# A two-direction state-space scan with MLP and attention: one four-column sum moved from VectorE to GpSimd, and the scan's last sums reordered on TensorE

## The reference

```
h = (x - mean) * rsqrt(var + 1e-5) * (1 + scale) + shift        # per token, modulated by the condition
for direction in (forward, backward in time):
    xs, z = split(h @ in_w); xs = silu(xs)
    proj = xs @ xproj_w;  dt = softplus(proj[:512] + bias);  B, C = proj[512:576], proj[576:640]
    for each time step:  state = state * exp(dt * A) + dt * xs * B        # 512 channels x 64 states
                         y = sum over the 64 states of state * C
    y = (y + xs * D) * silu(z) @ out_w
x = x + gate * (y_forward + y_backward)
x = x + gate * mlp(norm(x))                                     # then an attention layer with its own MLP
```

## Time and profile before

| what | value |
|---|---|
| median of 3 runs | 3260.04 us (3252.33 to 3261.91) |
| the profiled execution's own time | 3261.6 us |
| its span, first to last instruction | 3258.6 us |
| TensorE matmul busy | 3193.8 us (98%) |
| VectorE busy | 2771.5 us (85%) |
| ScalarE busy | 2679.6 us (82%) |
| GpSimd busy | 2448.3 us (75%) |
| mean granted TensorE clock | 0.994 |

### The profile page before, as it was taken

The page is one execution under the profiler, slowest core; times in us unless marked ns, Lnnn a source line. Parts: engine busy times, 40 slices in busy tenths (PEclk is TensorE's granted clock), DMA queues, the critical chain, the costliest instruction groups (busy, mean ns, idle before and its releaser), DMA issues. The chain is left out here.

```text
span 3258.6 us, 60423 instructions
## 1 busy us (share of the span) xinstructions
PE 3193.8 (98%) x23784; PEld 2687.1 (82%) x23784; DVE 2771.5 (85%) x3073; ACT 2679.6 (82%) x4456; POOL 2448.3 (75%) x617
## 2 busy tenths in 40 slices
PE   8999999999999999999999999999999999999999
PEld 6999899984699989997479999999648999888844
DVE  3999999966399999996659999999656999999861
ACT  4999999955699999994569999999357999999744
POOL 3999999950299999994039999999305999999800
PEclk9999999999999999999999999999999999999999
DMA  5222222210222222220022322222002222222100
GB/s 191 73 81 73 83 73 80 79 46 1 73 72 87 78 84 74 76 85 30 14 81 65 88 79 77 82 73 79 21 14 85 85 76 84 68 74 74 48 14 7
DMA packets 194235, 222.08 MB, mean 68 GB/s; under 512 B 77336, under 2 KB 149016, under 8 KB 193056
## 3 DMA queue, kind: packets, MB, share of 16 engines
q1 hardware_dynamic: 193952, 218.22, 22.1%
HBM read 213.70 MB, written 4.48 MB: 67 GB/s over the span
## 5 line engine op out<-in xcount | busy, mean ns | idle before, releaser
L621 POOL TENSOR_TENSOR states<-states,c_rows 128x2048 f32<-128x2048 f32 x336 | 1533.5, 4583 | 421.1 <-DVE states L1504 417.9
L1504 DVE TENSOR_TENSOR_SCAN states<-decay,bank 128x512 f32<-128x512 f32 x1376 | 1580.8, 1203 | 124.9 <-PE bank L1025 105.9
L771 ACT ACTIVATE decay<-dt,a_log 128x512 f32<-128x512 f32 x2048 | 1308.5, 712 | 0.0
L765 ACT ACTIVATE inflow_tok<-dtx_tok,b_tok 128x512 f32<-128x512 f32 x1536 | 999.2, 715 | 127.5 <-PE bank L1025 121.9
L1024 PE MATMUL bank<-ident,inflow_tok 128*128 128x128 f32 x6144 | 1046.4, 279 | 33.4 <-DVE states L1504 19.2
L1024 PEld LDWEIGHTS bank<-ident,inflow_tok 128*128 128x128 f32 x6144 | 706.5, 141 | 206.1 <-issue 72.1
L1044 PE MATMUL bank<-ident,states 128*128 128x128 f32 x5504 | 825.5, 273 | 4.1 <-DVE y_gated L1510 3.0
L1025 PE MATMUL bank<-b_diag,dtx_tok 128*128 128x128 f32 x4096 | 794.0, 276 | 0.0
L1504 DVE TENSOR_TENSOR_SCAN y_gated<-decay,bank 128x512 f32<-128x512 f32 x672 | 778.2, 1203 | 17.4 <-ACT decay L771 5.0
L621 POOL TENSOR_TENSOR y_gated<-y_gated,c_rows 128x2048 f32<-128x2048 f32 x168 | 770.2, 4584 | 27.9 <-DVE y_gated L1504 26.1
L1044 PEld LDWEIGHTS bank<-ident,states 128*128 128x128 f32 x5504 | 646.3, 142 | 10.5 <-DVE y_gated L1510 5.3
(11 more groups left out here) (161 smaller groups left out, 2238.9 us busy)
## 6 DMA issues: line engine op xcount, KB each, us to landing
c_rows<-c_spill SPq DMA_DIRECT2D x256, 512.0 KB, 3.7
b_diag<-diag_ring SPq DMA_DIRECT2D x256, 128.0 KB, 2.2
xproj_w<-in_xproj_w SPq DMA_DIRECT2D x32, 320.0 KB, 4.1
in_w<-in_in_w SPq DMA_DIRECT2D x16, 512.0 KB, 4.8
in_w<-in_fc_w SPq DMA_DIRECT2D x8, 512.0 KB, 4.4
xproj_w<-in_w SPq DMA_DIRECT2D x8, 512.0 KB, 4.5
xproj_w<-in_fc_w SPq DMA_DIRECT2D x4, 1024.0 KB, 5.3
x_ahead<-in_x SPq DMA_DIRECT2D x4, 512.0 KB, 6.6
```

The costliest lines, as they stand in the source:

```text
L621: pool.tensor_tensor(state_row, state_row, c_row.to_broadcast([P, KI, L]), ALU.mult).then_inc(weighed, PAIRS)
L765: last_tok = act.activation(inflow_tok[:, r % SLOTS, t, :], dtx_tok[:, d, t, :], ACT.Copy, scale=b_tok[:, d, t, s:s + 1])
L771: act.activation(decay[:, r % SLOTS * KI + k, :], dt[:, d, k, :], ACT.Exp, scale=a_neg[:, d, k, s:s + 1]).then_inc(decay_ready, 1)
L1504: dve.tensor_tensor_scan(state_slots[r % STATES][:, k, time], decay[:, slot, time], banks[k % INFLOW_BANKS][:, time], 0.0, ALU.mult, ALU.a ...
```

## The change

It has two parts. The look-ahead's sum of variance and epsilon leaves VectorE's `look_ahead` and is issued by GpSimd's `look_ahead` at the same step number, 16, with the wait for the four aggregates before it. And at the scan's end TensorE's order becomes: two of the four products of `project(0, 0)`, the last step's four `sum_up`, the other two products of `project(0, 0)`, then for each t `turn_high(t)` followed by one product of `project(0, 1)`, then `project(1, t)` as before. The first piece of the diff is in GpSimd's block, the next two in TensorE's, the last in VectorE's.

```
             def look_ahead(b, s):
 
+                if s == AHEAD_VAR_AT:
+                    pool.wait_ge(ahead_aggr, (b + 1) * TT)
+                    pool.tensor_scalar(var_eps[:], mean_var[:, :, 1], EPS_MAMBA, None, ALU.add).then_inc(ahead_var, 1)
                 if s == AHEAD_POWER_AT:
...
-            def project(d, t):
-                for k in range(KI):
+            def project(d, t, tiles=range(KI)):
+                for k in tiles:
                     last = pe.matmul(banks[t][:, 0:D], y_chan[d][:, k, t * P:(t + 1) * P], out_w[:, d, k, :],
...
-                project(0, 0)
-                sum_up(b, r, 0)
-                sum_up(b, r, 1)
-                sum_up(b, r, 2)
-                sum_up(b, r, 3)
-                project(0, 1)
+                project(0, 0, range(0, PAIR))
+                for k in range(KI):
+                    sum_up(b, r, k)
+                project(0, 0, range(PAIR, KI))
                 for t in range(TT):
                     turn_high(b, t)
+                    project(0, 1, (t,))
                 for t in range(TT):
                     pe.wait_ge(y_high_ready, b * TT + t + 1)
                     project(1, t)
...
-                if s == AHEAD_VAR_AT:
-                    dve.wait_ge(ahead_aggr, (b + 1) * TT)
-                    dve.tensor_scalar(var_eps[:], mean_var[:, :, 1], EPS_MAMBA, None, ALU.add).then_inc(ahead_var, 1)
```

## The result

| | before | after |
|---|---|---|
| median of the runs, us | 3260.34 (20 runs, 3252.33 to 3267.41) | 3249.85 (20 runs, 3244.45 to 3255.50) |
| the profiled execution, us | 3261.6 | 3253.48 |
| its span, us | 3258.6 | 3251.7 |
| ratio after / before | | 0.9967, 95% interval 0.9960 to 0.9973 |

The changed kernel is 10.5 us faster by the medians, and 8.8 to 13.0 us by the interval (3260.34 times 0.0027 and 0.0040). The interval lies on both sides of the border of 0.3% that the prediction drew (a ratio of 0.9970): that the kernel is faster is clear, that it is so by more than 0.3% is not.

A forecast was written before the change was run, and what follows sets the result against it. TensorE, busy 98% of the span, was taken to bound the kernel, with VectorE and GpSimd nearly as full. Terms -11.3 + 0 + 1.1 = -10.2 us, from the median 3260.04, gave 3249.8 us, range 3245 to 3256.

The forecast's parts named there:

- the border of 0.3%: Line between faster and the same: a measurement can tell about 0.3%, 9.8 us, from no change; it lies at 3250.3 us.
- Term 1, the gap: Steps 16 to 22, forward: taking the sum off VectorE saves 3.75 us in each of three samples, 11.3 us.
- Term 2, the sum on GpSimd: Step 16, between two GpSimd products: the sum takes 0.2 us, covered by idle time, so 0 us.
- The idle time of 0.33: GpSimd's idle time in us per step before its products, said to cover the sum's 0.2 us.
- the upper end of 1.04: Longest duration in us allowed for the sum on GpSimd, from the four-column power; said to stay covered.
- GpSimd then has no idle time for many steps: Behind step 16, if the sum takes its upper end: GpSimd's backlog is 0.7 us, with step 24 the tightest row.
- The rival in which GpSimd becomes the bound: Sum held on GpSimd for 2.25 us, TensorE waits about 1 us in each of three samples: 3252.8 us; chance 0.06.
- Term 3, the scan's end: TensorE's new order at four scan ends gains nothing and makes the first turn wait: 1.1 us lost, ends 0 and 2.0.
- The rival in which the end pays 0.86 each: Each of four scan ends gives back 0.86 us and no wait arises: 3245.3 us; chance 0.10.
- a wait that costs the clock: At each of four scan ends the wait drops TensorE to half clock, costing 3.75 us: 3263.7 us; chance 0.04.
- Only VectorE's own time returns: In the scan, only 2.25 us a sample comes back, 6.8 us in all: 3254.3 us; chance 0.12.
- The split between faster and the same: Outcome chances around 3250.3 us: faster 0.50, same 0.46; the forecast's 0.68 was divided into 0.40 and 0.28.

The follow-up runs named there:

- e3: Kernel before, with the sum still on VectorE but placed behind the scan of tile 3 of step 16: 3250.84 us, ratio 0.9968.
- e4: Kernel before, with the sum still on VectorE but placed between the scans of tiles 0 and 1 of step 16: 3265.81 us, ratio 1.0017.
- Four sums: Changed kernel with 3 more unread sums on GpSimd ahead of the real one: 3250.64 us, ratio 0.9965 to the kernel before.
- e1: Kernel before with only the sum moved to GpSimd, TensorE's order as before: 3250.09 us, ratio 0.9973.
- e7: Changed kernel with 11 more unread sums on GpSimd ahead of the real one, twelve in all: 3257.63 us, ratio 0.9994 to the kernel before.

## Why the prediction was right

**Term 1, the gap (11.3 us; ends 6.8 and 12.7).** The mechanism held at each point: no VectorE op of this line is held in the scan, the idle 2.5 us is gone, the clock is 1.00, and steps 16 to 22 take 29.17 us where 29.2 was said. Where the sum stays on VectorE but meets no product (e3), the same gain appears, and where it meets more of one (e4), the loss grows. The size was taken from one profiled execution in which the clock fell behind all three gaps. It is 2.15 us a gap without a fall and 3.75 with one; with 10 falls in 15 the term is 3 x (2.15 + 1.6 x 0.67) = 9.7 us, with 8 in 9 it is 10.7. This step read a chance as a constant, and by 0.6 to 1.6 us too high; 11.3 happened to stay inside the interval.

**Term 2, the sum on GpSimd (0.2 us, at no cost).** It takes 0.23 to 0.27. The price is near, and so is the cover: the first of two products in the row below ends near 996.0, and TensorE sums it from 996.81, which leaves 0.8, where 0.9 was seen before.

```profile
991.47 9.10 POOL L624 TENSOR_TENSOR states<-states,c_rows 128x2048 f32<-128x2048 f32 x2
```

```profile
996.81 0.60 PE L1047 MATMUL bank<-ident,states 128*128 128x128 f32 x4
```

TensorE shows no wait for GpSimd in steps 18 to 31 of a forward direction. The idle time of 0.33 was read off one product and is the longest of its neighbours: four in a row, from 935.59 on in the kernel before, show 0.29, 0.25, 0.18 and 0.33. Four sums (1.07 us) cost nothing, as was said of the upper end of 1.04. "GpSimd then has no idle time for many steps" shows itself with twelve, where the last wait is for step 24's product. The rival in which GpSimd becomes the bound is refuted for the change and true from somewhere between 1.1 and 3.5 us. The Trainium skill, GPSIMD Engine Reference, section Engine selection, would keep an elementwise op on VectorE. By that rule the sum was well placed, and the runs here say the opposite, 2.23 us held there against 0.24 on GpSimd. The rule's factor of 2 is given for ops with two inputs; this sum has one, so the 0.34 that the prediction drew from it does not follow.

**Term 3, the scan's end (1.1 us lost).** The abutting pieces told the truth: no gain, and a first turn that is late. It is late by 0.14 and not 0.2, and in the fourth sample GpSimd costs 0.1 and not 0.3, so the term is 4 x 0.14 + 0.1, or 0.7 us. The rival in which the end pays 0.86 each is refuted by 7.10 against 6.95; the reorder alone supports that, as its interval ends at -3.3 us, just short of the rival's -3.4. The one on the other side, a wait that costs the clock, needed 2.8 us an end; the longest wait that the reorder alone shows there is 0.31, a ninth of it.

**The sum.** With the terms as measured it is -9.7 or -10.7, plus 0.7: 9.0 to 10.0 us, against 10.5 measured (8.8 to 13.0). "Only VectorE's own time returns" would have given 3254.3, 4.5 us above what was measured; its 6.8 is nevertheless close to what the gaps cost without the clock, 6.5. The split between faster and the same was drawn at 3250.3, in the middle of the forecast's own range, and the measured interval has that border inside it too: the runs don't decide between the two outcomes to which the prediction gave 0.50 and 0.46. That the time lay 0.05 us from the forecast is luck, since a single execution scatters by 5 us to either side.

What stays open: no run beats the changed kernel beyond what the intervals tell, and e1, e3 and the full change can't be told apart by their times. What decides whether the clock falls behind a single gap is not known. Nor was it measured whether one GpSimd instruction for both the sum and the power would save more (e5_fused has no result).

## What to carry to other kernels

Look at the minimum, the median and the maximum of a tiny VectorE op: if they are 0.17 and 2.2 us, the op is held, and comparing its end with the end of GpSimd's instruction says by whom. Put such an op where GpSimd idles, or give it to GpSimd if the rows there show some slack; either gave all that was to be had here. Price a TensorE gap by the same steps in a stretch without the suspected part, over several executions and not one, since the clock behind it may or may not fall; and where pieces abut in the chain, another order of the same work gives nothing and uses up cover.

## What the runs showed of the hardware that was not expected

- The same gap of 2.44 to 2.49 us on TensorE was followed by the 1.2 GHz level (granted clock 0.51, 0.50 and 0.54 in the three stretches shown) in 10 of 15 cases and by an unchanged 1.00 in the others. It made the gap's price 3.6 to 3.8 us or 2.1 to 2.2. The three of 3.45 to 3.49 us in e4 were all followed by a fall (0.64 over 4.7 us); those of up to 0.85 us in e7 were not.
- A VectorE tensor-scalar of four columns was held for the whole rest of a GpSimd product (2.25 and 3.65 us, 0.14 where it met none), while four aggregates of VectorE inside such a product took 0.35 us together.
- A four-column tensor-scalar on GpSimd takes 0.22 to 0.27 us, with 0.30 for each of a row in which one waits for the other (3.26 over 11). The estimate by the columns of larger ones gave 0.02 us, so what is fixed in it is most of it.
